# First attention: first scores copied out of PSUM bank by bank, each bank handed back by itself

## What is computed

```python
def _L0_attn_ref(x, Wq1, Wk1, Wq2, Wk2, Wv, Wout):
    ...
    q1, k1 = (_apply_rotary(q1, cos, sin), _apply_rotary(k1, cos, sin))
    q2, k2 = (_apply_rotary(q2, cos, sin), _apply_rotary(k2, cos, sin))
    s1 = jnp.einsum('bqhd,bkhd->bhqk', q1, k1)
    s2 = jnp.einsum('bqhd,bkhd->bhqk', q2, k2)
    causal = jnp.tril(jnp.ones((T, T), dtype=bool))
    pattern = jnp.where(causal[None, None], s1 / D * (s2 / D), 0.0)
    y = jnp.einsum('bhqk,bkhd->bqhd', pattern, v).reshape(B, T, C)
    return y @ Wout.T
...
x = x + s * g      # s: attention of the layer, g: silu of its mixture of experts; twice
```

## Time and profile before

| | |
|---|---|
| median of three runs | 1788.18 us |
| profiled execution | 1787.87 us |
| its span | 1786.5 us |
| TensorE matmuls busy | 1641.2 us (92%) |
| VectorE busy | 990.2 us (55%) |
| ScalarE busy | 977.7 us (55%) |
| GpSimd busy | 828.1 us (46%) |
| copies of the first scores (L784) | 192, mean 1024 ns, 196.5 us |
| score matmuls (L1581) | 1536 records, 222.6 us busy, 37.5 us idle before them |

### The profile page before, as it was taken

The page is one execution under the profiler, slowest core; times in us unless marked ns, Lnnn a source line. Parts: engine busy times, 40 slices in busy tenths (PEclk is TensorE's granted clock), DMA queues, the critical chain, the costliest instruction groups (busy, mean ns, idle before and its releaser), DMA issues.

```text
span 1786.5 us, 49361 instructions
## 1 busy us (share of the span) xinstructions
PE 1641.2 (92%) x19349; PEld 1176.7 (66%) x19353; DVE 990.2 (55%) x2079; ACT 977.7 (55%) x1851; POOL 828.1 (46%) x906
## 2 busy tenths in 40 slices
PE   7899999999988999999999899888889999999996
PEld 5444444444446998998787566555557999986664
DVE  6688798777773222222999676344443222227775
ACT  5666666666664444444555465545544444446673
POOL 6233577777773545453122102555553555542322
PEclk9999999999999999999999899999999999999999
DMA  9900003000014777774342100111112232314332
GB/s 338 381 2 2 10 28 95 28 25 28 27 35 140 221 231 210 228 220 140 104 136 74 51 3 14 37 35 36 37 36 68 85 96 83 97 49 118 97 97 67
DMA packets 172420, 170.02 MB, mean 95 GB/s; under 512 B 20800, under 2 KB 139584, under 8 KB 169248
## 3 DMA queue, kind: packets, MB, share of 16 engines
q1 hardware_dynamic: 151440, 128.76, 24.0%
q0 software_dynamic: 16832, 34.64, 5.6%
q10 hardware_dynamic: 3920, 3.46, 0.7%
HBM read 97.16 MB, written 69.63 MB: 93 GB/s over the span
## 4 chain that ended last, share of the span: by engine, by line
PE 81%; issue 6%; DVE 5%; ACT 3%; DMA 2%; SPq 2%; POOL 0%; another core or an unknown queue 0%; ACTq 0%; DVEq 0%; POOLq 0%
PE ps L1787 12%; PE ps L1581 12%; PE ps L1778 11%; PE ps L1605 5%; PE ps L1543 4%; PE ps L1737 4%; PE ps L1709 4%; PE ps L1741 4%; PE ps L1672 4%; PE ps L1826 3%; PE ps L1814 3%; PE ps L1544 3%; PE ps L1718 2%; ACT s_PX L850 2%; DMA s_X<-xd 2%
## 5 line engine op out<-in xcount | busy, mean ns | idle before, releaser
L594 POOL DMA_INDIRECT xd<-s_XN,s_slots x256 | 250.2, 977 | 146.2 <-PE ps L1741 57.4
L784 ACT ACTIVATE s_S<-ps 128x1024 f32<-128x1024 f32 x192 | 196.5, 1024 | 179.4 <-PE ps L1581 177.0
L1444 DVE TENSOR_TENSOR s_PP<-ps,s_S 128x1024 f32<-128x1024 f32 x192 | 234.7, 1222 | 100.4 <-PE ps L1581 69.1
L1581 PE MATMUL ps<-s_QM,s_KK 32*128 32x512 f32 x1536 | 222.6, 645 | 37.5 <-issue 31.8
L850 ACT ACTIVATE s_PX<-ps,s_scl 128x1024 f32<-128x1024 f32 x128 | 135.6, 1110 | 217.9 <-PE ps L1718 217.9
L1294 DVE TENSOR_REDUCE s_RS<-ps 128x8 f32<-128x1024 f32 x128 | 150.8, 1217 | 154.0 <-PE ps L1676 111.5
L627 POOL TENSOR_SCALAR_AFFINE_SELECT s_S<-s_S 128x1024 f32<-128x1024 f32 x128 | 139.8, 1092 | 145.1 <-ACT s_S L784 142.5
L611 POOL DMA_INDIRECT yd<-s_Y,s_to x142 | 135.9, 957 | 147.5 <-DVE s_to L1381 102.2
L865 ACT ACTIVATE s_HH<-ps,s_LG 128x256 f32<-128x256 f32 x284 | 123.5, 473 | 146.6 <-PE ps L1778 131.6
L611 POOL DMA_INDIRECT yd<-s_XN,s_to x128 | 122.5, 957 | 129.9 <-DVE s_to L1381 102.7
L865 ACT ACTIVATE s_XN<-ps,s_b1s 128x256 f32<-128x256 f32 x256 | 113.1, 473 | 126.4 <-PE ps L1778 120.2
(11 more groups left out here) (220 smaller groups left out, 3047.1 us busy)
## 6 DMA issues: line engine op xcount, KB each, us to landing
s_W<-in_up_w SPq DMA_DIRECT2D x71, 256.0 KB
s_W<-in_down_w SPq DMA_DIRECT2D x71, 256.0 KB
s_X<-xd SPq DMA_DIRECT2D x135, 132.0 KB
xd<-s_zero SPq DMA_DIRECT2D x16, 1056.0 KB, 18.1
s_YG<-yd SPq DMA_DIRECT2D x32, 256.0 KB, 3.5
s_XN<-yd SPq DMA_DIRECT2D x32, 256.0 KB, 4.0
yd<-s_zero SPq DMA_DIRECT2D x7, 1056.0 KB, 27.5
s_DBt<-in_down_b SPq DMA_DIRECT2D x71, 64.0 KB
```

The lines of the kernel that those rows point to most:

```text
L594: e.indirect_dma_start(out=xd, out_offset=bass.IndirectOffsetOnAxis(ap=m.slots[:, k, i:i + 1], axis=0), in_=m.XNp[:, i, 0:C + 1], in_offse ...
L784: e.mul(m.S1[u % 3][:], m.PA, 1.0 / 64.0).then_inc(s.ev1, 1)
L1444: e.tensor_tensor(m.PP[u % 4][:], m.PB[u % 2], m.S1[u % 3][:], ALU.mult).then_inc(s.prod, 1)
L1581: return e.matmul(out, m.KK[k][32 * r:32 * r + 32, kind, kc * P:(kc + 1) * P], m.QM[k][32 * r:32 * r + 32, kind, :, qc * P:(qc + 1) * P], ...
```

## The change

`first_scores_copy` makes two copies of 512 columns, one for each bank of `m.PA`. Each waits for its own half of the first scores and increments `ev1`. Every first-scores matmul now increments `sc1`. In `score_units` the wait on `ev1` moves from the head of the group to the place ahead of each of the two first-scores matmuls: ahead of bank 0 it is for the copy of bank 0, ahead of bank 1 for that of bank 1. Counts that used `sc1` and `ev1` elsewhere are doubled: the wait in `query_masks` and `rotate` (12 in place of 6 for a sequence), in `causal`, and in VectorE's product at v = 2 and 3.

```diff
 def causal(e, m, s, u):
     sel = m.S1[u % 3][:].rearrange("p (b q) -> p b q", q=P)
-    e.wait_ge(s.ev1, u + 1)
+    e.wait_ge(s.ev1, 2 * u + 2)
...
     if b >= 2:
-        e.wait_ge((s.sc1, s.sc2)[kind], 6 * (b - 1))
+        e.wait_ge((s.sc1, s.sc2)[kind], (12, 6)[kind] * (b - 1))
...
 def first_scores_copy(e, m, s, u):
-    e.wait_ge(s.sc1, u + 1)
-    if u >= 3:
-        e.wait_ge(s.prod, u - 2)
-    e.mul(m.S1[u % 3][:], m.PA, 1.0 / 64.0).then_inc(s.ev1, 1)
+
+    for t in range(2):
+        e.wait_ge(s.sc1, 2 * u + t + 1)
+        if u >= 3:
+            e.wait_ge(s.prod, u - 2)
+        e.mul(m.S1[u % 3][:, t * 512:(t + 1) * 512], m.PA[:, t * 512:(t + 1) * 512], 1.0 / 64.0).then_inc(s.ev1, 1)
...
             if v in (2, 3):
-                e.wait_ge(s.ev1, u + 1)
+                e.wait_ge(s.ev1, 2 * u + 2)
...
         e.wait_ge(s.qm, 2 * b + 1)
         e.wait_ge(s.ka, 2 * b + 1)
-        if w >= 1:
-            e.wait_ge(s.ev1, w)
...
     for t in range(2):
         if w < NU:
-            i = scores(w, 0, t)
-            if t == 1:
-                i.then_inc(s.sc1, 1)
+            if w >= 1:
+                e.wait_ge(s.ev1, 2 * w - 1 + t)
+            scores(w, 0, t).then_inc(s.sc1, 1)
         if u >= 0:
             i = scores(u, 1, t)
             if t == 1:
```

## The result

The changed kernel took **1775.25 us** (median of 5 runs, 1770.08 to 1777.71) beside 1788.18 for the kernel before: a ratio of 0.9925, 95% interval 0.9896 to 0.9953; the medians are 12.9 us apart. The prediction said 1774, 1764 to 1784, and faster. The profiled execution took 1770.08 (span 1768.8), 17.8 less than the profiled one of before.

The account below looks back on a forecast made before the run. The first attention's copy-paced units were taken to be bound by the bank pair's 2.41 us round; 57 pairs at 0.24 us give 13.7, so 1787.9 - 13.7 = 1774.2, written 1774, range 1764 to 1784.

Parts of the forecast that it names:

- What bounds the kernel: The change acts only in the first attention's 192 units, 496 us; the bank pair's copy round of 2.41 us paces most.
- TensorE ready at 2.08 and 2.13: After a score group's start, TensorE could begin the next at 2.08 us (value products between) or 2.13 (projection between).
- The round by hand: Two copy-paced units of the first attention take 4.59 us in place of 4.82; the gain comes every second unit.
- C's start: Start of bank 1's first-scores product: bank 1 copied out at 2.26 us, plus 0.20 lag, so 2.46.
- What VectorE would do: VectorE's product follows bank 1's second scores; in units 2.13 behind their forerunner it is 0.22 us late, made up next unit.
- TensorE's idle time ahead of L1581: Sign of being right: TensorE's 31.8 us idle in 114 waits before score matmuls halves, in half as many waits.
- Places 5 and 0 still 2.70: Sign of being right: the two TensorE-paced units in each batch of six keep their 2.70 us.
- Rival 1: Late bank 1 products wait behind bank 0 products' second passes, 0.51 us; a pair gains 0.10, total 1782; chance 0.17 (shared).
- Rival 2: The wait before bank 1's products cuts all 192 score groups in two, 0.51 us each: slower, 1846; chance 0.12.
- Rival 3: The two ScalarE copies take 1.3 us in place of 1.07, so the change does nothing: 1788; chance 0.08.
- Rival 4: More comes back: all 31.8 us idle plus 0.07 at each of 114 starts, 39.8, to 1748; chance 0.08 (below 1769).
- The additional increment at nothing: One more TensorE increment per score group, possibly 0 to 5.7 us over 114 copy-paced starts, was taken as costing nothing.

Follow-up runs that it names:

- the last experiments: The changed kernel with GpSimd's scatters per unit at (0, 2, 1, 1, 1, 1) in place of (1, 1, 2, 1, 1, 0): 0.9876 of the kernel before.

## Why the prediction was right, point by point

**What bounds the kernel: right.** The gain lies in the first attention alone: its last score matmul began 17 us earlier in the profiled execution (531.8 against 548.8), some 2.5 of them by the clock in the first batch, and of the 1237 us behind it TensorE was busy 1148 before and 1150 after.

**The copies: right.** 595 ns each, 1.08 to 1.09 a pair where 1.07 was taken.

**TensorE ready at 2.08 and 2.13: right.** Place 1 is followed after 2.08 in 30 of 32 batches, place 3 in 26.

**The round by hand: the mechanism right, one term mis-sized.** The play of two units, the first start at 2.08 with a late C, the next with all four together, is what the trace shows, in the first pair of most batches at places 1 and 2 and in the second at 3 and 4, where that is not stretched. The term that failed is C's start, "bank 1 is out at 2.26; C and D start at 2.46". The 0.20 was the lag of a whole group in before. The runs with the moved waits show 0.06 of it to be the wait instruction behind the late one, 0.06 more the wait instruction in which the late one stood, and 0.03 the way from the weight load to the first matmul of a group that finds TensorE idle; C's wait sits on its weight load and other matmuls run, and its lag is 0.05. So C comes 0.21 behind A, not 0.38; the pair takes 2.08 + 2.33 = 4.41 in place of 4.59, and saves 0.41 in place of 0.24. With 57 pairs that is 23.4 us, and 1764.5, at the very edge of the range.

**What was not seen: the stretched groups.** Twenty of them lose about 0.4 us each (2.73 in place of 2.33): 8 us. 23.4 − 8 = 15.4. The 30 whole batches behind the first, whose clock differed, took 461.2 before and 448.0 after, 13.2 less (446.6 in the second trace of the changed kernel). Most of the 2 us between is what the four batches of the next paragraph did not gain. The two errors, 0.17 a pair too little gained and 8 us of stretches not foreseen, have opposite signs and nearly cancel. **The number was right for a reason that was half right, and that it came out within 1.3 us is luck**; had scatters and copies been placed otherwise, the same working would have missed by 8 us or more, as the last experiments show (0.9876, where the prediction's 13.7 us would be 0.9923).

**What VectorE would do: right where named, incomplete elsewhere.** At place 3 its product is 0.21 late (309.91 where the group's modelled end is 309.70), 0.22 predicted, and nobody waits for it. But in the batches in which VectorE also does the routing between units it ends last once TensorE is faster. The timeline of the changed kernel there:

```profile
252.57 1.22 DVE L1446 TENSOR_TENSOR s_PP<-ps,s_S 128x1024 f32<-128x1024 f32 x1
253.70 0.68 DVE L1235 TENSOR_TENSOR s_RT<-ps,s_cs 128x512 f32<-128x512 f32 x1
...
254.53 0.67 PE L1545 MATMUL ps<-s_XT,s_W 128*128 128x256 f32 x2 [0.53 <-DVE s_RT L1235]
```

TensorE's projection waits 0.53 for VectorE's rotation. The four batches of that kind (the 12th to the 15th) went from 15.43 only to 15.05 to 15.10 us, though two pairs, 0.82, were there to be had. They take 15.05 without scatters too, so this is not the stretches' doing. A product of VectorE that ends last was one of the signs of being wrong that the prediction named. In before's table of waits it was there to be found, in small: TensorE ahead of the projection for VectorE's rotation, 2.9 us in 3 waits; in the changed kernel it is 6.9 us in 8.

**TensorE's idle time ahead of L1581: wrong as an indicator.** "Halved, in half as many waits" was expected; it fell to 5.3 us. A late C is no idle time, as A and B run. An indicator that sees only the first matmul of a group can't count a wait inside it; the distance from group to group can.

**Places 5 and 0 still 2.70: right**, 2.71 both.

**Rival 1 (C behind A's second pass) fell.** C starts 0.21 behind A, at 306.44, and A's second pass comes at 306.76, 0.53 behind A. **Rival 2 (every group cut) fell** with it: where bank 1 is long free all four start together, and such groups have 1.14 as in before. By the Trainium skill ("TensorE: Matmul & The Clock Gate", "The mechanism") matmuls start and end strictly in program order; neither trace agrees, since C overtakes the second pass of A that stands ahead of it. **Rival 3 (nothing) fell** with copies of 595 ns. **Rival 4 (more comes back)** had the wrong bound: "half of it, 1768, is the most that I can see" rested on the same 0.20. With the scatters out of the way the attention gave back 24 to 25 us (485.7 to 461.3; without scatters 484.7 to 459.6), 1 us of either by the clock in the first batch, so some 23 to 24 of the 39.8. With a lag of 0.05 for C the working itself would have given 1764.5 and made this rival the forecast; the 0.55 for the forecast's own case came out by the second error.

**The additional increment at nothing: right as far as it can be seen.** With two copies, two increments and everything else as before, the round is 2.42 against 2.41. The Trainium skill (same page, "The cost: per-tile semaphore tail") gives 26 ns for each; the round of this run is 10 ns longer with the copies' 0.06 in it, and its copies start 0.05 earlier, as they wait for A alone; so such a tail is not seen here, and would have to lie in the shadow of B to D. The 0.32% of the whole run, some 6 us with an interval of 2 to 10, doesn't exclude 26 ns in each of the 192 groups.

## What to carry to other kernels

When a wait is met just in time, look at what stands between it and the instruction that it guards: put the wait that comes last last; here each wait instruction behind it cost 0.06 us a round (one moved line gave 0.46% of this kernel). Handing back a buffer in parts gains where the first part lets the engine start on time, and then the lag of the *last* part decides; take it from how that wait stands in the program, not from the lag of the old one. And once an engine runs without reserve, look for what comes at the same moment on engines that seemed to have no part in it: here placing the same scatters behind other units gave about two thirds as much again as the change, by ratios from two chips.

## What the runs showed of the hardware

- **In a group with a wait inside, TensorE can stop issuing for a while near the end of a GpSimd scatter.** In the group of 310.64 of the changed kernel three weight loads are issued, then for 0.30 us none runs, then the other five come from 311.23 on. The fourth has no wait for a copy ahead of it, so it is not C's wait that holds it. GpSimd in the same kernel:

```profile
309.46 0.95 POOL L594 DMA_INDIRECT xd<-s_XN,s_slots  x1 [0.30 <-issue]
310.87 1.09 POOL L627 TENSOR_SCALAR_AFFINE_SELECT s_S<-s_S 128x1024 f32<-128x1024 f32 x1 [0.46 <-issue]
```

  The scatter ended at 310.41; TensorE's issue goes on about 0.8 us behind that. So it does in 15 of the 20 groups (0.76 to 0.82); in three, in which the scatter ends inside the group, it goes on 0.36 to 0.39 behind it, and in the 13 at place 2 with one scatter a unit 0.32 to 0.37. Shown by runs: without scatters there is no stretch at place 4 or 2; with the scatters moved the stretches move or go; the kernel before has none at places 1 to 4 with or without them. Not shown: what it is that TensorE's issue then lacks. Not every scatter does it: behind 103 of the 128 in the changed kernel, and 86 in before, TensorE issued something between 0.35 and 0.75 us after the scatter's end. That it takes a wait just met, and nothing queued ahead, is an inference: four kernels with a wait inside the group (the changed one, the same with one scatter a unit, and the two with the second scores first) have 13 to 20 stretched groups, and those whose groups wait as a whole have one at most at place 4 (with two copies one each, with one copy none).
- **A wait instruction whose marks are long there still takes time in TensorE's program**: 51 ns in the records, which can hold two of the program's waits; from the copy's end to the matmul 0.206 with one more wait instruction behind the late one, 0.144 with the late one in the last wait instruction, 0.05 where it sits on the weight load itself.
- **Two 128x512 copies from PSUM cost ScalarE 0.06 to 0.07 more than one of 128x1024** (1.08 or 1.09 against 1.02), though the two have 595 ns each: they overlap by 0.1.
